# A six-layer decoder on one core: attention heads taken four at a time instead of two, and a new table of ticks

## The chip, the cores and the metric

The kernel runs on one core of a Trainium2 chip. The metric is the device time of one execution in microseconds. The five engines are named as the profile does: PE (TensorE), DVE (VectorE), ACT (ScalarE), POOL (GpSimd) and SP (SyncE, which here only issues transfers). Each runs its own list of instructions in order, and they meet at semaphores.

## The reference, cut to what matters

A batch of 8 sequences of 256 tokens and 256 features passes a memory read and a cross attention (the front, left alone by the change) and then six layers of this:

```
for i in range(6):
    x = attn_layer(shift_tokens(x), Wqkv[i], q_scale[i], k_scale[i], Wo[i]) + x
    x = ffn_layer(shift_tokens(x), ln_g[i], ln_b[i], W1[i], b1[i], W2[i], b2[i]) + x

attn_layer: q, k, v = split(x @ Wqkv)              # 16 heads of 64
            q, k = l2norm(q) * qs, l2norm(k) * ksc, then rotary tables
            sim = q . k * 8 within a window of 64 and the one before it
            out = softmax(masked sim) @ v;  out @ Wo
ffn_layer:  xn = layernorm(x) * g + b
            a, gate = split(xn @ W1 + b1)          # 682 columns each
            a * gelu(gate) @ W2 + b2
```

Everything is float32. A product with weights is made of three passes over a high and a low part of both factors (PASSES).

## The kernel before, in words

`layers` walks over 48 steps (6 layers times 8 sequences) and two at the ends. One step is a **slot**, and each slot n is a pipeline over three sequences: the 16 heads of step n are attended, the feed-forward part (FFN) of step n-1 is computed, and the second half of the projections of step n (group 1) and the first half of those of step n+1 (group 0) are made. A group is 8 heads, 512 columns.

A slot has 16 **ticks**, one for each head. In every engine's `slot` function a tick t first does its share of the heads and then walks over `SCHEDULE[t]`, a table written out by hand, whose items each engine turns into its own instructions in `dense`. So SCHEDULE sets the order on PE, ACT, DVE and POOL at once, and nothing is reordered at run time. The items:

- `("unit", g, u)`: one product of 512 columns for group g, on PE into one of two `project` banks (L791). u 0 to 3 are q and k of two token tiles; ACT squares and copies them out (L949, L950). u 4 and 5 are v (L954).
- `("rotate", g, u)`: DVE sums the squares, applies the tables (L1134 to L1141), POOL takes a power and, for k, scales (L1050 to L1059).
- `("turn", g, u)`: PE transposes the rotated q or k into a `project` bank, ACT copies it to qT or kT (L963). "unit" and "turn" and "input" take the two banks in turn, and PE waits in `bank_free` until ACT has read the use before last.
- `("project_out", t)`: the output projection of one token tile (L821). `("add_out",)`: DVE adds the residual (L1146); SP then shifts the tokens by three transfers.
- `norm_stats`, `norm_apply`, `norm_turn`: the layer norm. `("input",)`: the next sequence is transposed (L774), split by ACT and DVE.
- `("gate", i)`, `("value", i)`: a third of W1's gates or values each, into the single bank `wide` (L844). ACT applies Gelu to the gates (L982), DVE multiplies the values in (L1179), ACT makes the high part hT (L991 to L994), which is a single buffer and therefore waits until PE has made `("down", i-1)` from it (L859); `("low", i)` is its low part on DVE. `("residual",)`: L1195.

A head's own way, before the change, at tick t: at even t PE makes the scores of heads t and t+1 (`pair_scores`, L878, two banks, one for each side of a pair); DVE masks head t with the running minimum (L1215) at tick t; ACT takes the exponentials with their sums (L1019) in the same tick; at t+1 DVE inverts the sum (L1205) and scales (L1223); PE transposes a pair at each odd tick (`turn_pair`, L891), ACT copies it to probsT (L1004); at even ticks PE mixes the pair of two steps earlier with v (`pair_mix`, L905 to L909), ACT copies it to oT (L1012) and DVE makes its low part (L1228).

Gelu and the exponential are in different tables of ACT, so each slot loads a table twice (ACT_TABLE_LOAD at L982 and at L1019).

## Time and profile before

| | us |
|---|---|
| median of 3 runs | 3348.35 (3347.62 to 3349.45) |
| the profiled execution's own time | 3347.67 |
| its span | 3345.9 |
| busy in the span: PE, DVE, ACT, POOL | 2950.3, 2440.5, 2211.5, 1464.3 |
| mean granted clock of PE | 0.974 of 2.4 GHz |
| one slot in steady state | 62.4 |

The span runs from the first to the last instruction, so 1.8 us of the profiled execution lie around it. An engine's busy time counts its instructions; the rest is waiting. The idle time that stands with an instruction is what its engine waited just before it, and the name behind the arrow is the one that ended the wait. The chain that ended last has 44% on PE, 27% on DVE, 11% on ACT and 11% of issue.

### The profile page before, as it was taken

The numbers are of one execution on the slowest core, as the hardware profiler recorded it, in microseconds if no ns is written. First come the engines' busy times: TensorE is split into PE (matmuls) and PEld (weight loads), VectorE is DVE, ScalarE is ACT, GpSimd is POOL, SyncE is SP. The second block draws the span as 40 slices with busy tenths as digits, with TensorE's granted clock in tenths as the row PEclk, the third lists the DMA queues.
The fourth block names the chain that finished last, engine by engine and source line by source line (L and its number), as shares of the span: only waits on it lengthen the run. The fifth ranks groups of instructions, "written<-read, shape, count | busy, mean of one in ns | idle before, by whom it ended". The sixth has DMA issues, their size and how long they took to land.

```text
span 3345.9 us, 83253 instructions
## 1 busy us (share of the span) xinstructions
PE 2950.3 (88%) x26408; PEld 2463.4 (74%) x26408; DVE 2440.5 (73%) x8851; ACT 2211.5 (66%) x6256; POOL 1464.3 (44%) x1052
## 2 busy tenths in 40 slices
PE   6778998888999888999988999988999988898996
PEld 5567877777777767777776777766777767777775
DVE  3477777777777777777777777777777777777773
ACT  3357667666676666767666766766676666667663
POOL 3354454334444444445443444433544543454450
PEclk9899999999999999999999999999999999999997
DMA  4210010111001111100112010012101011110000
GB/s 136 68 40 23 17 30 22 40 57 53 22 17 30 42 50 49 30 22 17 30 53 71 18 30 22 17 40 76 35 20 27 24 41 48 35 32 27 27 26 21
DMA packets 109664, 124.10 MB, mean 37 GB/s; under 512 B 11589, under 2 KB 84129, under 8 KB 109473
## 3 DMA queue, kind: packets, MB, share of 16 engines
q1 hardware_dynamic: 109472, 121.75, 12.7%
q8 instruction: 95, 1.56, 0.2%
q14 instruction: 97, 0.79, 0.1%
HBM read 73.50 MB, written 16.78 MB: 27 GB/s over the span
## 4 chain that ended last, share of the span: by engine, by line
PE 44%; DVE 27%; ACT 11%; issue 11%; DMA 2%; DVEq 1%; POOL 1%; SPq 0%; ACTq 0%; POOLq 0%
PE project L791 12%; PE wide L844 7%; DVE with_sin L1137 6%; PE acc L859 6%; PE score L878 5%; DVE sums_sq L1134 4%; PE acc L821 4%; DVE probs L1215 4%; DVE probs L1223 3%; PE turned L891 2%; PE mix L905 2%; DVE sums_sq L1139 2%; ACT L982 2%; ACT with_sin L949 2%; ACT probs L1019 2%
## 5 line engine op out<-in xcount | busy, mean ns | idle before, releaser
L791 PE MATMUL project<-w_qkv,xT 128*128 128x512 f32 x3456 | 953.3, 415 | 37.8 <-DVE xT L1117 33.8
L1050 POOL TENSOR_TENSOR query_scale<-sums_sq,half 128x8 f32<-128x8 f32 x192 | 412.9, 2151 | 1230.8 <-DVE sums_sq L1139 1225.8
L1019 ACT ACTIVATE probs<-probs,shift 128x128 f32<-128x128 f32 x1536 | 605.4, 396 | 430.5 <-DVE shift L1215 425.2
L791 PEld LDWEIGHTS project<-w_qkv,xT 128*128 128x128 f32 x3456 | 628.2, 194 | 172.7 <-DVE xT L1117 41.9
L1215 DVE CUSTOM_DVE_ANT_0 probs<-score,mask,query_scale 128x128 f32<-128x128 f32 x1536 | 468.7, 342 | 304.1 <-PE score L878 290.3
L844 PE MATMUL wide<-nT,w_up 128*128 128x256 f32 x3456 | 493.6, 293 | 149.2 <-ACT gates L982 87.5
L844 PEld LDWEIGHTS wide<-nT,w_up 128*128 128x128 f32 x3456 | 444.5, 194 | 201.9 <-ACT gates L982 108.9
L1053 POOL TENSOR_TENSOR inv_norm<-sums_sq,half 128x8 f32<-128x8 f32 x192 | 411.2, 2141 | 224.5 <-DVE sums_sq L1139 223.1
L1223 DVE TENSOR_SCALAR probs<-probs,inv_sums 128x128 f32<-128x128 f32 x1536 | 381.5, 291 | 0.0
L1134 DVE TENSOR_REDUCE sums_sq<-with_sin 128x8 f32<-128x512 f32 x384 | 261.8, 682 | 78.8 <-ACT with_cos L950 78.6
L1137 DVE TENSOR_TENSOR with_sin<-with_cos,tables 128x512 f32<-128x512 f32 x384 | 301.9, 786 | 13.3
L878 PE MATMUL score<-kT,qT 64*64 64x128 f32 x6144 | 258.2, 283 | 53.7 <-DVE shift L1215 42.5
L1012 ACT CAST oT<-mix 128x256 fp32r<-128x256 f32 x384 | 143.8, 374 | 242.4 <-PE acc L821 142.3
L821 PE MATMUL acc<-w_out,oT 128*128 128x256 f32 x2304 | 296.3, 284 | 1.0 <-issue 1.0
L878 PEld LDWEIGHTS score<-kT,qT 64*64 64x64 f32 x6144 | 167.1, 133 | 167.4 <-issue 160.9
L1019 ACT ACTIVATION_READ_ACCUMULATOR probs<-probs,shift 128x1 f32 x1536 | 289.9, 189 | 0.0
L891 PE MATMUL turned<-ident,probs 128*128 128x128 f32 x1536 | 241.5, 280 | 44.9 <-DVE probs L1223 39.5
L821 PEld LDWEIGHTS acc<-w_out,oT 128*128 128x128 f32 x2304 | 277.1, 189 | 4.7 <-issue 1.2
L949 ACT ACTIVATE with_sin<-project 128x512 f32<-128x512 f32 x384 | 227.2, 592 | 76.5 <-PE project L791 76.5
L1141 DVE TENSOR_TENSOR with_cos<-with_cos,tables 128x512 f32<-128x512 f32 x384 | 265.9, 692 | 13.1
L859 PE MATMUL acc<-w_down,hT 128*128 128x256 f32 (+1 forms) x1728 | 246.1, 288 | 15.5 <-DVE hT L1190 11.2
L1004 ACT COPY probsT<-turned 128x512 f32<-128x512 f32 x384 | 226.1, 589 | 46.6 <-issue 39.9
(121 smaller groups left out, 5099.3 us busy)
## 6 DMA issues: line engine op xcount, KB each, us to landing
v_mid<-v SPq DMA_DIRECT2D x192, 128.0 KB, 2.3
staging<-in_w_qkv SPq DMA_DIRECT2D x24, 768.0 KB
y_in<-y_scratch SPq DMA_DIRECT2D x48, 256.0 KB, 2.8
res<-y_scratch SPq DMA_DIRECT2D x48, 256.0 KB, 2.7
y_scratch<-res SPq DMA_DIRECT2D x40, 256.0 KB, 2.4
staging<-in_w_up SPq DMA_DIRECT2D x12, 682.0 KB
staging<-in_w_out SPq DMA_DIRECT2D x6, 1024.0 KB
xn<-res SPq DMA_DIRECT2D x48, 112.0 KB, 2.3
```

The costliest lines, as they stand in the source:

```text
L791: last = pe.matmul(project[(x - 1) % 2][:], xT[a][:, h, t * P:(t + 1) * P], w_qkv[w][:, h, c, g, :], start=(h == 0 and (a, w) == PASSES[0] ...
L821: last = pe.matmul(acc[:, t, :], oT[a][:, p, t * P:(t + 1) * P], w_out[w][:, p, :], start=(p == 0 and (a, w) == PASSES[0]), stop=(p == PAI ...
L844: last = pe.matmul(wide[:, k, :], w_up[w][:, h, col:col + P], xnT[a][:, h, :], start=(h == 0 and (a, w) == PASSES[0]), stop=(h == HALVES - ...
L859: last = pe.matmul(acc[:, t, :], hT[a][0:rows, k, t * P:(t + 1) * P], w_down[w][0:rows, j, :], start=(j == 0 and t == 0 and (a, w) == PASS ...
L878: last = pe.matmul(score[side][sides[w % 2], (w // 2) * P:(w // 2 + 1) * P], qT[rows, pair, w * WINDOW:(w + 1) * WINDOW], kT[rows, pair, f ...
L1019: last = act.activation(probs[:, t % 4, cols], probs[:, t % 4, cols], ACT.Exp, bias=shift[:, t % 2, i:i + 1], scale=-1.0, accum_out=sums[: ...
L1050: pool.tensor_tensor(query_scale[:, u // 2, g * GROUP_HEADS:(g + 1) * GROUP_HEADS], sums_sq[:, u, :], half[:, 0:GROUP_HEADS], ALU.pow).the ...
L1053: pool.tensor_tensor(inv_norm[:, u // 2, :], sums_sq[:, u, :], half[:, 0:GROUP_HEADS], ALU.pow)
L1134: dve.tensor_reduce(sums_sq[:, u, :], with_sin[:, u, :].rearrange("p (h d) -> p h d", h=GROUP_HEADS), AXIS_X, ALU.add).then_inc(squares_su ...
L1137: dve.tensor_tensor(heads(with_sin[:, u, :]), heads(with_cos[:, u, :])[:, :, ::-1, :], table(2 * c + 1), ALU.mult)
L1215: last = dve.tensor_tensor_reduce(out=probs[:, t % 4, a:b], in0=score[t % 2][:, a:b], in1=mask[:, a:b], scale=query_scale[:, i, t:t + 1], ...
L1223: last = dve.tensor_scalar(probs[:, h4, a:b], probs[:, h4, a:b], inv_sums[:, h4, i:i + 1], None, ALU.mult)
```

## The change

1. **Heads in fours.** At every fourth tick PE makes the scores of four heads (`quad_scores`) and mixes the four heads before them (`quad_mix`). With q = t % 4: DVE masks heads 0 and 1 of the four at q = 0 and heads 2 and 3 at q = 1; ACT takes their exponentials in the same ticks; DVE scales 0 and 1 at q = 1, and 2 and 3 at q = 2; PE transposes 0 and 1 at q = 2 and 2 and 3 at q = 3. The four go to oT in one copy of 512 columns, at q = 0 on ACT and at q = 1 on DVE; the sums of two heads are inverted in one instruction. probsT holds four heads, shift four.
2. **A new SCHEDULE**, in which the output projection moves from ticks 3 and 4 to 1 and 2, the layer norm two ticks ahead, the gates from tick 9 to tick 7, and the rest with them.
3. **w_up without padding between its halves**, which pays for the larger probsT: the last tile of gates reads on into the next half, in rows that are not used later.
4. In SP's list the load of the tables at a layer's end moves behind the three shifting transfers.

```diff
 SCHEDULE = {
     0: [("unit", 1, 0)],
-    1: [("rotate", 1, 0), ("unit", 1, 1), ("rotate", 1, 1), ("unit", 1, 2)],
-    2: [("unit", 1, 3), ("rotate", 1, 2), ("turn", 1, 0)],
-    3: [("rotate", 1, 3), ("project_out", 0), ("turn", 1, 1)],
-    4: [("project_out", 1), ("turn", 1, 2), ("add_out",)],
-    5: [("unit", 1, 4)],
-    6: [("turn", 1, 3), ("unit", 1, 5), ("norm_stats",), ("input",)],
-    7: [("unit", 0, 0), ("norm_apply",)],
-    8: [("rotate", 0, 0), ("norm_turn",)],
-    9: [("unit", 0, 1), ("gate", 0), ("rotate", 0, 1), ("unit", 0, 2), ("gate", 1), ("unit", 0, 3), ("gate", 2)],
-    10: [("rotate", 0, 2), ("turn", 0, 0)],
-    11: [("value", 0), ("rotate", 0, 3), ("turn", 0, 1), ("unit", 0, 4), ("low", 0)],
-    12: [("value", 1), ("down", 0), ("turn", 0, 2), ("low", 1)],
-    13: [("value", 2), ("down", 1), ("turn", 0, 3), ("low", 2)],
-    14: [("down", 2)],
-    15: [("unit", 0, 5), ("residual",)],
+    1: [("unit", 1, 1), ("rotate", 1, 0), ("project_out", 0)],
+    2: [("rotate", 1, 1), ("project_out", 1), ("unit", 1, 2)],
+    3: [("add_out",), ("rotate", 1, 2), ("unit", 1, 3), ("turn", 1, 0)],
+    4: [("norm_stats",), ("rotate", 1, 3), ("turn", 1, 1)],
+    5: [("unit", 1, 4), ("norm_apply",), ("unit", 1, 5), ("turn", 1, 2)],
+    6: [("norm_turn",), ("turn", 1, 3), ("input",), ("unit", 0, 0)],
+    7: [("gate", 0), ("unit", 0, 1), ("gate", 1), ("rotate", 0, 0), ("gate", 2)],
+    8: [("rotate", 0, 1), ("unit", 0, 2)],
+    9: [("value", 0), ("unit", 0, 3)],
+    10: [("rotate", 0, 2), ("value", 1), ("turn", 0, 0), ("low", 0)],
+    11: [("down", 0), ("value", 2), ("rotate", 0, 3), ("turn", 0, 1), ("low", 1)],
+    12: [("low", 2), ("turn", 0, 2)],
+    13: [("down", 1), ("unit", 0, 4)],
+    14: [("down", 2), ("turn", 0, 3), ("unit", 0, 5)],
+    15: [("residual",)],
 }
...
-                    if t % 2 == 0 and s.head(t, 0) is not None:
-                        pair_scores(s, t, s.head(t, 0))
-                    if t % 2 == 0 and s.head(t, 4) is not None:
-                        pair_mix(s.n, (t - 4) % HEADS, s.head(t, 4), s.n * PAIRS + (t - 4) // 2)
-                    if t % 2 == 1 and s.head(t, 2) is not None:
-                        turn_pair((t - 2) % HEADS, s.head(t, 2))
+                    q = t % QUAD_HEADS
+                    if q == 0 and s.head(t, 0) is not None:
+                        quad_scores(s, t, s.head(t, 0))
+                    if q == 0 and s.head(t, 4) is not None:
+                        quad_mix(s.n, (t - 4) % HEADS, s.head(t, 4), s.n * PAIRS + (t - 4) // 2)
+                    if q == 2 and s.head(t, 2) is not None:
+                        turn_pair(0, s.head(t, 2))
+                    if q == 3 and s.head(t, 3) is not None:
+                        turn_pair(2, s.head(t, 3) + 2)
...
+                    k = 2 * (q % 2)
+                    H = s.head(t, q)
+                    if H is not None and q < 2:
+                        for j in range(k, k + 2):
+                            act.wait_ge(scores_masked, H + j + 1)
...
+                            last.then_inc(exp_done, 1)
+                    if H is not None and q >= 2:
+                        act.wait_ge(probs_turned, H + k + 2)
+                        wait(act, mixed, H)
+                        act.copy(probsT[:, k:k + 2, :].rearrange("p a b -> p (a b)"), turned[:]).then_inc(probsT_copied, 2)
...
-                        act.copy(oT[0][:, pair, :], mix[:, pair % 2, :]).then_inc(out_high, 1)
+                        act.copy(oT[0][:, pair:pair + 2, :], mix[:]).then_inc(out_high, 2)
...
+                    if H is not None and q in (1, 2):
+                        dve.wait_ge(exp_done, H + done + 2)
+                        dve.reciprocal(inv_sums[:, done:done + 2, :], sums[:, done:done + 2, :]).then_inc(sums_inverted, 2)
+                    if H is not None and q < 2:
...
+                        dve.wait_ge(scores_ready, H + QUAD_HEADS)
+                        wait(dve, probs_turned, H)
+                        for k in (2 * q, 2 * q + 1):
...
+                            last.then_inc(scores_masked, 1)
+                    if H is not None and q in (1, 2):
...
+                    if q == 1 and s.head(t, 5) is not None:
+                        pair = ((t - 5) % HEADS) // 2
+                        dve.wait_ge(out_high, s.n * PAIRS + (t - 5) // 2 + 2)
+                        dve.tensor_tensor(oT[1][:, pair:pair + 2, :], mix[:], oT[0][:, pair:pair + 2, :].bitcast(FP32),
+                                          ALU.subtract).then_inc(out_split, 2)
```

How the order moves, first on ACT at ticks 5 and 6 (exponentials, then v out of its banks, then qT). Before, tick 5 and the start of tick 6:

```order
L1019 ACTIVATE probs,sums<-probs,shift 128x128 [waits scores_masked]
L1019 ACTIVATE probs,sums<-probs,shift 128x128
L942 REGISTER_ALU
L954 COPY v<-project 128x512 [waits mixed,filled]
L1012 CAST oT<-mix 128x256 [waits mixed]
```

With the change, tick 5:

```order
L1018 ACTIVATE probs,sums<-probs,shift 128x128 [waits scores_masked]
L1018 ACTIVATE probs,sums<-probs,shift 128x128
L1015 REGISTER_ALU
L1018 ACTIVATE probs,sums<-probs,shift 128x128 [waits scores_masked]
L1018 ACTIVATE probs,sums<-probs,shift 128x128
L951 REGISTER_ALU
L963 COPY v<-project 128x512 [waits mixed,filled]
L951 REGISTER_ALU
L963 COPY v<-project 128x512 [waits mixed,filled]
L968 REGISTER_ALU
L972 COPY qT<-project 128x4x128 [waits scores_ready,filled]
```

Two heads' exponentials, and no longer one head's, stand ahead of the copy of v, and the second v and a turn stand in the same tick.

Second, PE at the same place, ticks 5 and 6 with the change (the two units of v, then "turn" 1, 2, then a pair of heads turned, the norm's transposes):

```order
L795 MATMUL project<-w_qkv,xT 128x512 [waits act_read]
L795 MATMUL project<-w_qkv,xT 128x512 x5
L95 REGISTER_ALU
L795 MATMUL project<-w_qkv,xT 128x512 [waits act_read]
L795 MATMUL project<-w_qkv,xT 128x512 x5
L804 REGISTER_ALU
L95 REGISTER_ALU [waits parts_ready]
L813 MATMUL project<-ident,with_cos 128x128 [waits act_read]
L814 MATMUL project<-ident,with_sin 128x128
```

Before, a score, a mix and a turned pair of heads stood around a single unit at this place:

```order
L891 MATMUL turned<-ident,probs 128x128 x3
L93 REGISTER_ALU
L791 MATMUL project<-w_qkv,xT 128x512 [waits act_read]
L791 MATMUL project<-w_qkv,xT 128x512 x5
L93 REGISTER_ALU
L878 MATMUL score<-kT,qT 64x128 [waits scores_masked]
L878 MATMUL score<-kT,qT 64x128 x7
```

So "turn" 1, 2 is now the third use of a bank in a row, and waits for a read that ACT makes after four activations.

Third, ACT at ticks 11 to 12, the cast of the last third of hT and what follows it. Before, ticks 13 and 14:

```order
L993 CAST hT<-gates 128x256 [waits h_used]
L994 CAST hT<-gates 42x256
L959 REGISTER_ALU
L963 COPY kT<-project 128x4x128 [waits scores_ready,filled]
L1012 CAST oT<-mix 128x256 [waits mixed]
```

With the change:

```order
L1002 CAST hT<-gates 128x256 [waits h_used]
L1003 CAST hT<-gates 42x256
L968 REGISTER_ALU
L972 COPY kT<-project 128x4x128 [waits scores_ready,filled]
L1015 REGISTER_ALU
L1018 ACTIVATE probs,sums<-probs,shift 128x128 [waits scores_masked]
L1018 ACTIVATE probs,sums<-probs,shift 128x128
```

The cast waits on h_used, which PE gives after ("down", 1). Before, that item was in the same tick as the cast (13); now the cast is in tick 11 and ("down", 1) in tick 13, behind a score, a mix and a turn.

## Rows read from the trace of the kernel before

**Rows 1.** The page's first part: busy time and share of PE.

```profile
PE 2950.3 (88%) x26408; PEld 2463.4 (74%) x26408; DVE 2440.5 (73%) x8851; ACT 2211.5 (66%) x6256; POOL 1464.3 (44%) x1052
```

**Rows 2.** One steady slot: stretch, its length, busy of each engine, PEclk, DMA, GB/s.

```profile
1501.30:1563.70 62.40, 57.81 (x541) 48.56 (x540) 47.49 (x179) 43.64 (x125) 29.16 (x20) 1.00 0.09 23
```

**Rows 3.** Timeline of DVE, the residual additions alone: start, us, line, operation.

```profile
604.99 0.69 DVE L1195 TENSOR_TENSOR res<-acc,res 128x512 f32<-128x512 f32 x1
...
820.89 0.68 DVE L1195 TENSOR_TENSOR res<-acc,res 128x512 f32<-128x512 f32 x1
...
1472.11 0.68 DVE L1195 TENSOR_TENSOR res<-acc,res 128x512 f32<-128x512 f32 x1
...
1534.51 0.69 DVE L1195 TENSOR_TENSOR res<-acc,res 128x512 f32<-128x512 f32 x1
```

**Rows 4.** Timeline of PE: start, us, what, and the idle time before it with its releaser.

```profile
1506.60 1.68 PE L844 MATMUL wide<-nT,w_up 128*128 128x256 f32 x12 [1.19 <-DVE nT L1169]
...
1511.04 1.69 PE L844 MATMUL wide<-nT,w_up 128*128 128x256 f32 x12 [1.37 <-ACT gates L982]
```

**Rows 5.** Timeline of PE where it waits for nothing: starts show what each takes.

```profile
1535.56 0.67 PE L878 MATMUL score<-kT,qT 64*64 64x128 f32 x16
1536.16 0.44 PE L905 MATMUL mix<-probsT,v 128*64 128x128 f32 x4
...
1536.76 1.66 PE L791 MATMUL project<-w_qkv,xT 128*128 128x512 f32 x6
1538.25 0.60 PE L891 MATMUL turned<-ident,probs 128*128 128x128 f32 x4
...
1545.55 3.06 PE L821 MATMUL acc<-w_out,oT 128*128 128x256 f32 x24
```

**Rows 6.** Timeline of ACT behind the unit of rows 5.

```profile
1538.53 0.60 ACT L949 ACTIVATE with_sin<-project 128x512 f32<-128x512 f32 x1 [0.47 <-PE project L791]
1539.02 0.58 ACT L950 COPY with_cos<-project 128x512 f32<-128x512 f32 x1
...
1539.97 0.42 ACT L1019 ACTIVATE probs<-probs,shift 128x128 f32<-128x128 f32 x1
...
1540.75 0.60 ACT L949 ACTIVATE with_sin<-project 128x512 f32<-128x512 f32 x1
```

**Rows 7.** Timeline of DVE: values, a head masked and scaled, rotations, norm statistics.

```profile
1520.76 0.87 DVE L1179 SCALAR_TENSOR_TENSOR gates<-wide,params,gates 128x256 f32<-128x256 f32 x2
...
1536.52 0.35 DVE L1215 CUSTOM_DVE_ANT_0 probs<-score,mask,query_scale 128x128 f32<-128x128 f32 x1 [0.65 <-PE score L878]
...
1537.07 0.48 DVE L1223 TENSOR_SCALAR probs<-probs,inv_sums 128x128 f32<-128x128 f32 x2
1537.46 0.42 DVE L1228 TENSOR_TENSOR oT<-mix,oT 128x256 fp32r<-128x256 f32 x1
...
1539.64 0.69 DVE L1134 TENSOR_REDUCE sums_sq<-with_sin 128x8 f32<-128x512 f32 x1 [0.17 <-ACT with_cos L950]
...
1541.86 0.69 DVE L1134 TENSOR_REDUCE sums_sq<-with_sin 128x8 f32<-128x512 f32 x1
...
1559.16 0.29 DVE L1153 BATCH_NORM_STATS2 ln_stats<-res 128x6 f32<-128x128 f32 x1 [0.18 <-DMA xn<-res]
```

**Rows 8.** Timeline of ACT: the table load and the first two Gelu.

```profile
1508.85 1.28 ACT L982 ACT_TABLE_LOAD   x1
1510.15 0.84 ACT L982 ACTIVATE gates<-wide,params 128x256 f32<-128x256 f32 x2
```

**Rows 9.** Timeline of ACT: the last third of hT.

```profile
1530.24 0.41 ACT L993 CAST hT<-gates 128x256 fp32r<-128x256 f32 x1 [0.53 <-PE acc L859]
```

**Rows 10.** Timeline of PE: the same forms as in rows 4 and 5 behind longer waits.

```profile
219.06 0.89 PE L806 MATMUL project<-ident,with_cos 128*128 128x128 f32 x4 [2.12 <-POOL with_cos L1059]
...
724.32 2.79 PE L844 MATMUL wide<-nT,w_up 128*128 128x256 f32 x12 [2.57 <-ACT gates L982]
...
755.62 1.13 PE L878 MATMUL score<-kT,qT 64*64 64x128 f32 x16 [2.53 <-ACT v L954]
```

127 lines of the change are left out of this document (56 added, 71 removed).

## The prediction, made before the changed kernel was run

> **What bounds the kernel now.** I read the page first. PE is busy in 88% of the span, DVE in 73%, ACT in 66% [rows 1]. Then the stretches: in a steady slot of 62.4 us PE is busy for 57.8 at the full granted clock, DVE for 47.5 and ACT for 43.6 [rows 2]. Then the timeline of PE, which repeats from slot to slot: the residual additions are 62.4 apart [rows 3]. What PE issues without waiting is read from the starts [rows 5]: scores of a pair of heads 0.6, mix of a pair 0.6, a unit 1.5, a turned pair of heads 0.4, one tile of the output projection 2.9 (24 matmuls of 3.06 with the overlap taken off); the six groups of `wide` and three of `down` take 1.5 each (the first row of rows 4 with its overlap off). A slot has 12 units (17.9), 9 such groups (13.5), two projection tiles (5.8), 8 pairs scored and mixed (9.6), 8 turned (3.2), and 56 transposes of q, k, the input and the norm at 0.11, the rate of rows 5's turned pair (6.2): 56.2 us. So in each slot PE loses only 6.2 us, in short waits such as the 1.19 and 1.37 around the gates [rows 4] with what each drains. **PE bounds it, and a perfect order could give 10% at most.** DVE and ACT have 15 and 19 us of slack, but they are in order, so what matters is what stands ahead of the instruction that PE waits for.
>
> **What the edits save by themselves.** Per slot: four copies to oT of 512 columns for eight of 256, four subtractions likewise, eight inversions for sixteen. That is 1 to 2 us less on ACT and as much on DVE, beside PE, and nothing on PE, which issues the same matmuls. The missing padding of w_up and SP's moved load change no duration: the same 128 columns are read, and the table load is wanted only at a layer's end; cover gone, it would cost one transfer in five switches, under 3 us each. I take 0.
>
> **What the order does.** I walk one steady slot with these steps. DVE: a head masked 0.55, scaled 0.4, a rotation 2.2 (1539.64 to 1541.86), a value group 0.8, norm statistics 1.3 (estimate from six instructions of the kind shown), 512 columns subtracted 0.6 to 0.7 [rows 7, 3]. ACT: a head's exponentials 0.8, square and copy together 1.0, other copies of 512 columns 0.5 and 0.6 until seen [rows 6]. What PE makes is seen 0.3 after its last issue (rows 5's unit is issued by 1538.25, ACT starts at 1538.53 [rows 6]). Time 0 is where PE starts the scores of tick 0.
>
> Tick 1. The scores are seen at 1.5, heads 0 and 1 are masked by 2.6, ACT has their exponentials at 3.8. DVE then inverts, masks heads 2 and 3, scales 0 and 1, and only then makes the low part of oT: 6.7. PE has scored and mixed (2.4) and made two units (5.4) and waits there for ("project_out", 0): **1.3 us**. Before, this item came two ticks later and waited for nothing.
>
> Ticks 1 to 5. PE has 11.6 us from there to the end of the scores of tick 4 (two projection tiles, two units, two turned pairs, one turn, the scores), so 18.3. DVE idles meanwhile, since the unit of rotation 1,2 comes behind both projection tiles. Then everything is due at once. DVE: heads 4 and 5 masked (to 19.7), norm statistics (21.0), rotation 1,3 (23.2), inversion and head 6 masked, seen at 23.9. ACT: exponentials of 6 and 7 (25.5), and only then the copy of v out of unit 1,4: 26.2. PE has finished both units of v at 23.5 (0.5 lost for its bank) and needs that bank for ("turn", 1, 2): **2.7 us**, behind the 0.5.
>
> Ticks 5 to 7. The turn, a turned pair and the norm's transposes end at 27.9. ACT then copies a turned pair, makes the norm's two activations and cast (1.6), empties turn 1,3 and both input halves, with DVE subtracting, before unit 0,0 may start at 31.8. PE's own work in it is 0.9: **3.1 us** lost. Then gate 0; its Gelu needs the table load and 0.84 [rows 8]; with one unit between, PE waits 1.0, and for gate 2, with nothing between, 1.1: **2.1 us**. The same two places cost 1.37 and nothing before.
>
> Ticks 8 to 11. DVE masks two heads, rotates 0,1, masks two, scales two, makes oT's low part and then value 0, at 50.1 when the scores began at 41.9. PE waits 1.0 for value 1, and then 1.8 for ("down", 0), whose low part stands behind a rotation and value 1, and 0.3 for ("down", 1): **3.1 us**.
>
> Ticks 11 to 14. ACT casts the last third of hT only after ("down", 1). Such a wait was 0.53 when both were in one tick [rows 9]. Now PE makes the scores, the mix and a turn of tick 12 first, and DVE a rotation and the low part: `down` 1 ends at 63.5 as ACT sees it. Behind the cast on ACT stand turn 0,1 and the exponentials of heads 12 to 15, so PE waits 1.5 for a bank and 2.3 for the scaled heads 12 and 13: **3.8 us**.
>
> Sum: 16.5 us of waits beside 56.2 of work, **72.7 for a slot, 10.3 more than now**, at the full clock. The slot closes: at 72.7 the scores of the next can start, and DVE and ACT are free by then.
>
> **PE's clock.** The rows show that after 2.57 us without work a group of `wide` took 2.79 and not 1.69, after 2.53 the scores 1.13 and not 0.67, after 2.12 four transposes 0.89 and not 0.60 [rows 10, 4, 5]: the half level, 1.2 GHz. After waits to 1.4 nothing of the kind shows in steady slots, whose granted clock is 1.00 [rows 2]. The changed slot has 2.7 us without work in tick 5 and then some 5.5 us with little of it up to unit 0,0. At half rate the turn, the turned pair and the norm's transposes take 1.7 more, turn 1,3 and an input half 0.6, unit 0,0 1.4 and the pair behind it 0.4, all on the path: about 4 us, so 76.7. The wait of 2.3 in tick 14 may do the same to `down` 2 and what follows (2.5 more: 79.2).
> The Trainium skill, "TensorE: Matmul & The Clock Gate", section on HAM oscillation, says that a kernel whose PE waits between bursts falls to half rate and pays for it in each burst. By that rule every slot would pay the 4 us; without it the sum below would be 3825. The trace agrees where the waits are long (rows 10).
>
> **The sum.** From the first to the last residual addition there are 47 intervals: 30 of 62.4, 15 around the five layer switches (each three 215.9, 604.99 to 820.89 [rows 3]) and two at the end. I take 14.3 more for each of the 30 (429), 10.3 for each of the 15 (155; these already pay for a slow clock, as at 724.32 and 755.62 [rows 10]), and 13 for the start and the end together, where half of the work is missing (from below 0, from above twice 14). 3347.7 of the profiled execution + 597 = **3945 us**; the median of the runs shown is 0.7 above that execution, which changes nothing.
>
> **The rivals.**
> *The chain as walked, at full clock.* Against it stand rows 10, for it that the clock kept up through shorter waits. 45 x 10.3 + 13: 3825. Chance 0.18.
> *Two falls per slot.* 30 x 16.8 + 155 + 13: 4020; with the switches paying too, 4095. Chance 0.27.
> *The waits are shorter than walked.* A step may be overlapped that I put in a row; with half of the growth at full clock, 3590, with three quarters 3705. Chance 0.07.
> *PE stays the bound and the order helps.* This needs what the change seems made for: DVE and ACT free when PE asks, and the waits at gates all that is left. Its place is tick 5: if ACT emptied unit 1,4 before the exponentials of heads 6 and 7, and DVE rotated beside them. A slot would be 56.2 + 2.1 at the gates and about 1 for draining, 59.3: 3.1 less in 45 intervals, 3208. It decides from where the waits of a slot sum to under 6.2. For it speaks DVE's and ACT's slack [rows 2], against it that both are in order. Chance 0.06. That the change does nothing measurable I give 0.02: it moves every wait.
> My forecast, one fall per slot, has 0.40.
>
> **The range.** 3700 to 4095: from three quarters of the growth to two falls with the switches. Left out are most of the short-wait case, the faster one, and anything beyond two falls, somewhat under 0.2. A measurement of this kernel tells 0.2% (7 us) from no change. Faster 0.06, same 0.02, slower 0.92.
>
> **What would show it.** In the changed profile: residual additions about 77 apart; busy times of ACT and DVE within 3% of now; "turn" 1,2 of PE (L813) waiting 2 to 3 us for ACT's v; the cast of hT (L1002) waiting some 5 us for PE's acc, and not 0.5; the turned pair (L897) waiting about 2 for DVE; the output projection (L825) waiting 1 to 1.5 for oT; the gates waiting 1 us twice; the granted clock well under 1.00 in each slot after the turn of tick 5, at full level otherwise. The forecast is wrong if those waits are there but short, if the clock stays at 1.00, or if the period is below 62.4; then DVE's or ACT's steps overlap in a way that rows 6 and 7 don't show.

## The result and the profile after

| | before | after |
|---|---|---|
| median, us | 3347.98 (4 runs, 3344.40 to 3349.45) | 4112.62 (4 runs, 4104.88 to 4124.02) |
| ratio to before | | 1.2289, 95% interval 1.2254 to 1.2323 |
| span of the profiled execution | 3345.9 | 4105.4 |
| busy PE, DVE, ACT, POOL | 2950.3, 2440.5, 2211.5, 1464.3 | 3167.5, 2436.6, 2157.4, 1448.5 |
| mean granted clock | 0.974 | 0.904 |
| one steady slot (mean of 30) | 62.4 | 77.0 |
| three intervals at a switch of layers (mean of 5) | 214.0 | 272.3 |

The change made the kernel 23% slower. The forecast was 3945 with a range up to 4095: right in its direction, and too low by 168 us, so that the result lies outside the range.

The page's first part, which answers to [rows 1]. PE does the same 26408 matmuls and is busy 217 us longer; DVE and ACT do no more work than before.

```profile
PE 3167.5 (77%) x26408; PEld 2676.1 (65%) x26408; DVE 2436.6 (59%) x8275; ACT 2157.4 (53%) x6064; POOL 1448.5 (35%) x1052
```

The stretches of the changed kernel (stretch, length, busy of PE, PEld, DVE, ACT and POOL, granted clock, DMA share, GB/s): two steady slots, which answer to [rows 2], and the three intervals at the first switch.

```profile
2362.50:2440.20 77.70, 63.66 (x541) 53.87 (x541) 47.90 (x165) 42.46 (x121) 28.78 (x20) 0.92 0.07 19
2440.20:2516.00 75.80, 59.15 (x542) 49.53 (x541) 47.96 (x165) 42.36 (x121) 28.78 (x20) 0.98 0.07 19
692.50:792.50 100.00, 74.38 (x586) 63.39 (x586) 55.38 (x182) 50.48 (x136) 29.01 (x20) 0.81 0.11 34
792.50:884.40 91.90, 69.88 (x552) 59.98 (x544) 53.66 (x177) 48.03 (x133) 29.11 (x20) 0.81 0.17 52
884.40:969.80 85.40, 61.49 (x503) 52.52 (x496) 49.30 (x170) 41.90 (x121) 28.78 (x20) 0.86 0.13 38
```

The same three intervals in the kernel before, in the same columns:

```profile
605.00:682.40 77.40, 63.02 (x544) 51.81 (x543) 56.74 (x195) 50.23 (x139) 29.12 (x20) 0.94 0.15 44
682.40:754.00 71.60, 60.93 (x542) 50.28 (x541) 54.50 (x189) 48.90 (x137) 29.38 (x20) 0.97 0.21 66
754.00:820.90 66.90, 59.84 (x536) 49.99 (x537) 48.62 (x182) 44.14 (x128) 29.11 (x20) 0.95 0.18 51
```

In the two steady slots PE is busy 61.4 us on average, 3.6 more than in [rows 2] for the same matmuls, which is the slower clock, and idle for 15.4 against 4.6: 10.8 us of new waits. Over all 30 steady slots the two are 3.9 (61.7 against 57.9 busy) and 10.7 (15.3 against 4.6 idle). The timeline of DVE, residual additions alone, answers to [rows 3]:

```profile
692.48 0.69 DVE L1206 TENSOR_TENSOR res<-acc,res 128x512 f32<-128x512 f32 x1 [0.76 <-PE acc L863]
...
969.75 0.69 DVE L1206 TENSOR_TENSOR res<-acc,res 128x512 f32<-128x512 f32 x1 [2.37 <-PE acc L863]
...
2440.25 0.69 DVE L1206 TENSOR_TENSOR res<-acc,res 128x512 f32<-128x512 f32 x1 [0.76 <-PE acc L863]
...
2516.06 0.69 DVE L1206 TENSOR_TENSOR res<-acc,res 128x512 f32<-128x512 f32 x1 [0.88 <-PE acc L863]
```

The first pair spans a switch, 277.3 us where before had 215.9; the five switches take 277.3, 276.6, 272.4, 272.6 and 262.9. The account from the residual additions of both traces: 30 steady intervals grew by 14.6 (437), 15 at switches by 19.5 (292, that is 5 x 58.4), the first addition came 11.3 later, and the last two intervals are 126.1 and not 106.8 (19.3). The sum is 759.5, and so is the difference of the spans.

Now the waits of one steady slot, in the timeline of PE (start, us, what, idle time before it and its releaser). The scores of tick 0 start at 2366.22.

```profile
2372.94 3.10 PE L825 MATMUL acc<-w_out,oT 128*128 128x256 f32 x24 [1.58 <-DVE oT L1243]
...
2388.07 1.66 PE L795 MATMUL project<-w_qkv,xT 128*128 128x512 f32 x6 [0.57 <-ACT kT L972]
2392.03 0.33 PE L813 MATMUL project<-ident,with_cos 128*128 128x128 f32 x1 [2.30 <-ACT v L963]
...
2397.55 0.44 PE L778 MATMUL project<-ident,y_in 128*128 128x128 f32 x2 [1.15 <-ACT kT L972]
2399.09 2.50 PE L795 MATMUL project<-w_qkv,xT 128*128 128x512 f32 x6 [1.09 <-DVE xT L1128]
...
2406.47 1.70 PE L848 MATMUL wide<-nT,w_up 128*128 128x256 f32 x12 [0.89 <-ACT gates L991]
2409.09 1.68 PE L848 MATMUL wide<-nT,w_up 128*128 128x256 f32 x12 [0.93 <-ACT gates L991]
...
2418.45 0.66 PE L897 MATMUL turned<-ident,probs 128*128 128x128 f32 x4 [1.21 <-DVE probs L1238]
2419.84 2.76 PE L848 MATMUL wide<-nT,w_up 128*128 128x256 f32 x12 [0.73 <-DVE gates L1190]
...
2434.11 1.68 PE L795 MATMUL project<-w_qkv,xT 128*128 128x512 f32 x6 [1.28 <-ACT kT L972]
2437.95 0.66 PE L897 MATMUL turned<-ident,probs 128*128 128x128 f32 x4 [2.16 <-DVE probs L1238]
```

With one of 0.15 they sum to 14.04, all that PE is idle in this slot. A unit (`project<-w_qkv,xT` x6) takes 2.50 after the waits around tick 5, where 1.66 is the full rate, and a value group 2.76 and not 1.69 after those of ticks 9 and 10: half clock for most of each. The stretches around tick 5 show it (same columns as above):

```profile
2392.00:2396.00 4.00, 3.97 (x21) 3.67 (x22) 2.94 (x12) 2.29 (x5) 1.10 (x1) 0.59 0.29 66
2396.00:2400.00 4.00, 1.76 (x8) 1.11 (x7) 1.54 (x3) 2.11 (x5) 1.42 (x2) 0.93 0.00 0
2400.00:2404.00 4.00, 4.00 (x20) 3.51 (x20) 1.23 (x2) 1.56 (x3) 0.00 (x0) 0.63 0.00 0
```

### The profile page after: what moved, and what is told of

It reads as the page before. It is cut to its first block, busy times and chain, and to the rows that moved or that the text cites. A ratio compares the mean times of both kernels' runs of the same rounds, so it can differ in the third digit from the quotient of the medians.

```text
span 4105.4 us, 82137 instructions
## 1 busy us (share of the span) xinstructions
PE 3167.5 (77%) x26408; PEld 2676.1 (65%) x26408; DVE 2436.6 (59%) x8275; ACT 2157.4 (53%) x6064; POOL 1448.5 (35%) x1052
## 4 chain that ended last, share of the span: by engine, by line
PE 47%; DVE 25%; issue 12%; ACT 10%; DVEq 1%; POOL 1%; ACTq 0%; DMA 0%; SPq 0%; POOLq 0%
PE project L795 10%; PE wide L848 10%; PE acc L825 7%; PE acc L863 6%; DVE probs L1229 5%; PE turned L897 4%; DVE probs L1238 4%; ACT probs L1018 4%; PE score L885 3%; DVE with_sin L1148 3%; DVE sums_sq L1145 2%; DVE gates L1190 2%; DVE oT L1243 2%; PE project L813 2%; ACT gates L991 1%
## 5 line engine op out<-in xcount | busy, mean ns | idle before, releaser
L795 PE MATMUL project<-w_qkv,xT 128*128 128x512 f32 x3456 | 1006.8, 433 | 145.8 <-ACT kT L972 91.6
L795 PEld LDWEIGHTS project<-w_qkv,xT 128*128 128x128 f32 x3456 | 662.1, 204 | 314.1 <-ACT kT L972 121.4
L848 PE MATMUL wide<-nT,w_up 128*128 128x256 f32 x3456 | 534.6, 310 | 124.6 <-ACT gates L991 88.5
L848 PEld LDWEIGHTS wide<-nT,w_up 128*128 128x128 f32 x3456 | 488.7, 212 | 172.9 <-ACT gates L991 119.3
L897 PE MATMUL turned<-ident,probs 128*128 128x128 f32 x1536 | 285.0, 317 | 235.3 <-DVE probs L1238 235.2
L1238 DVE TENSOR_SCALAR probs<-probs,inv_sums 128x128 f32<-128x128 f32 x1536 | 430.0, 343 | 6.8
L897 PEld LDWEIGHTS turned<-ident,probs 128*128 128x128 f32 x1536 | 219.9, 165 | 308.2 <-DVE probs L1238 278.9
L1145 DVE TENSOR_REDUCE sums_sq<-with_sin 128x8 f32<-128x512 f32 x384 | 258.8, 674 | 272.6 <-ACT with_cos L959 272.6
L813 PE MATMUL project<-ident,with_cos 128*128 128x128 f32 x768 | 206.4, 303 | 113.0 <-ACT v L963 113.0
L863 PEld LDWEIGHTS acc<-w_down,hT 128*128 128x128 f32 (+1 forms) x1728 | 236.0, 204 | 82.1 <-DVE hT L1198 69.1
L1148 DVE TENSOR_TENSOR with_sin<-with_cos,tables 128x512 f32<-128x512 f32 x384 | 266.2, 693 | 13.3
```

The lines of the kernel that those rows point to most:

```text
L795: last = pe.matmul(project[(x - 1) % 2][:], xT[a][:, h, t * P:(t + 1) * P], w_qkv[w][:, h, c, g, :], start=(h == 0 and (a, w) == PASSES[0] ...
L848: last = pe.matmul(wide[:, k, :], w_up[w][:, h * W1_COLS + col:h * W1_COLS + col + P], xnT[a][:, h, :], start=(h == 0 and (a, w) == PASSES ...
L863: last = pe.matmul(acc[:, t, :], hT[a][0:rows, k, t * P:(t + 1) * P], w_down[w][0:rows, j, :], start=(j == 0 and t == 0 and (a, w) == PASS ...
L897: last = pe.transpose(turned[:, (TILES * side + i) * P:(TILES * side + i + 1) * P], pr[:, i * P:(i + 1) * P], ident[:])
L1145: dve.tensor_reduce(sums_sq[:, u, :], with_sin[:, u, :].rearrange("p (h d) -> p h d", h=GROUP_HEADS), AXIS_X, ALU.add).then_inc(squares_su ...
L1148: dve.tensor_tensor(heads(with_sin[:, u, :]), heads(with_cos[:, u, :])[:, :, ::-1, :], table(2 * c + 1), ALU.mult)
```

## The experiments

For each kernel the table gives what the residual additions of its trace say: a steady interval (mean of 30), three intervals at a switch (mean of 5), and the **excess** of these over three steady ones. Each is read from one trace, and the steady slots of the changed kernel differ by up to 3.7 us among themselves, so a few tenths between its variants say little.

| kernel | median | ratio, 95% interval | steady | switch | excess |
|---|---|---|---|---|---|
| before | 3347.98 | | 62.4 | 214.0 | 26.6 |
| after | 4112.62 | 1.2289 [1.2254, 1.2323] | 77.0 | 272.3 | 41.3 |
| e1, fours alone | 3711.92 | 1.1073 [1.1041, 1.1105] | 70.2 | 236.8 | 26.2 |
| e2, table alone | 3819.31 | 1.1393 [1.1360, 1.1426] | 72.3 | 245.7 | 28.9 |
| e3, PE kept busy | 4065.59 | 1.2128 [1.2092, 1.2163] | 76.4 | 267.1 | 37.8 |
| e4, cast late | 3925.99 | 1.1711 [1.1667, 1.1755] | 73.8 | 256.4 | 35.1 |
| e5, v early | 4135.11 | 1.2367 [1.2316, 1.2418] | 77.7 | 273.9 | 40.8 |
| e45, both | 3927.35 | 1.1746 [1.1696, 1.1795] | 73.8 | 255.9 | 34.6 |
| e6, after with thin splits | 4043.86 | 1.2094 [1.2034, 1.2155] | 77.7 | 257.2 | 24.2 |
| e7, before with thin splits | 3278.38 | 0.9805 [0.9754, 0.9855] | 62.4 | 200.4 | 13.1 |
| e8, projection later | 4140.60 | 1.2378 [1.2345, 1.2410] | 77.8 | 275.2 | 41.8 |
| e9, rotation last | 4015.16 | 1.2003 [1.1982, 1.2024] | 75.1 | 264.7 | 39.3 |
| e10, before with gates covered | 3333.11 | 0.9962 [0.9949, 0.9975] | 62.3 | 210.5 | 23.5 |
| e11, splits moved | 4068.18 | 1.2151 [1.2061, 1.2241] | 77.4 | 264.6 | 32.3 |

### Which part of the change costs: e1 and e2

**e1: heads in fours, the old table.** The changed kernel with the SCHEDULE of the kernel before.

> The changed kernel with the SCHEDULE of before; heads still in fours. If the new table makes the loss (my theory), most of the 765 us go: 3350 to 3600. If the grain of four heads makes it (rival), the time stays above 3900. In between both have a share.

Measured 3711.92, between the two, so both parts have a share. **e2: the new table, heads in pairs.** The kernel before with the new SCHEDULE, with these items where its pairs and its cast can use them, the ffn's splits from tick 13 on, and the moved load of the tables:

```diff
-    1: [("unit", 1, 1), ("rotate", 1, 0), ("project_out", 0)],
-    2: [("rotate", 1, 1), ("project_out", 1), ("unit", 1, 2)],
-    3: [("add_out",), ...
+    1: [("unit", 1, 1), ("rotate", 1, 0)],
+    2: [("rotate", 1, 1), ("unit", 1, 2)],
+    3: [("project_out", 0), ("project_out", 1), ("add_out",), ...
-    11: [("down", 0), ("value", 2), ...("low", 1)], 12: [("low", 2), ("turn", 0, 2)], 13: [("down", 1), ("unit", 0, 4)]
+    11: [("down", 0), ...("low", 1)], 12: [("turn", 0, 2)], 13: [("value", 2), ("down", 1), ("unit", 0, 4), ("low", 2)]
```

> The kernel of before, heads in pairs, with the new table as near as pairs allow: both output projections in tick 3 (the last pair's low part is ready only after tick 2), the value group 2 and its cast in tick 13 with down 1, the weight splits of the up projection from tick 13 on, the tables' load behind the shifts. If the table makes the loss: 3700 to 3950. If the fours make it: 3350 to 3500.

Measured 3819.31, in the range of "the table makes the loss". But each part costs alone, 7.8 and 9.8 us a slot; together 14.6. The reading, argued from the orders above: the fours put two heads' masks and exponentials ahead of whatever a tick's items need, the table puts those items where they are needed at once. With fours under the old table the gates wait, for DVE's norm and for Gelu; the timeline of PE in e1:

```profile
1656.57 1.67 PE L848 MATMUL wide<-nT,w_up 128*128 128x256 f32 x12 [2.56 <-DVE nT L1180]
...
1661.78 2.93 PE L848 MATMUL wide<-nT,w_up 128*128 128x256 f32 x12 [2.14 <-ACT gates L991]
```

With pairs under the new table the waits of tick 5 are there all the same; the timeline of PE in e2:

```profile
1086.05 0.33 PE L809 MATMUL project<-ident,with_cos 128*128 128x128 f32 x1 [2.18 <-ACT v L954]
1091.65 0.44 PE L774 MATMUL project<-ident,y_in 128*128 128x128 f32 x2 [2.08 <-ACT kT L963]
```

So the turn of tick 5 waits because of its place, not because of the fours. And the excess at a switch is that of the kernel before in e1 and near it in e2 (26.2 and 28.9): only both together raise it. (In e2 the ffn's splits stand later too; e4 below has fours, the table and the splits in those places, and its excess is 35.1.)

### What the clock costs: e3

The changed kernel with matmuls of no use, whose result is overwritten, in PE's gaps of ticks 5 and 6:

```diff
+            def filler(f, count):
+                pe.wait_ge(acc_read, f * 2 + 1 + 1)
+                for k in range(count):
+                    pe.matmul(acc[:, k % 2, :], oT[0][:, 0, 0:P], w_out[0][:, 0, :], start=True, stop=True)
...
+                    if s.ffn and (g, u) == (1, 2):
+                        filler(f, 18)
...
+                    if s.ffn:
+                        filler(f, 12)
```

> The changed kernel, where PE makes 18 more matmuls of 256 columns into the idle acc bank before turn 1,2 and 12 more before the input's transposes (results unused), some 2 and 1.5 us at full rate, inside the two long waits of ticks 5 and 6. If the half clock after those waits costs about 4 us a slot, the added work keeps the clock up and the time FALLS, by 2.5 to 4 us in each of some 45 slots: 3930 to 4010, a steady period of 73 to 74.5. If the clock is not the cost, nothing or worse: 4110 to 4200.

The time, 4065.59, is in neither range. The clock did stay up where it was filled (1.00 from 2360 to 2380 in e3): the turn waited 0.18 and not 2.30, and the unit behind the input takes 1.67 and not 2.50. But the slot fell by 0.6 only. The half clock behind the waits of ticks 9 and 10 is there as without filling, in about every second slot (2.85 here, 2.76 in the slot shown above). The timeline of PE in e3:

```profile
2365.30 0.33 PE L822 MATMUL project<-ident,with_cos 128*128 128x128 f32 x1 [0.18 <-ACT v L972]
...
2371.91 1.67 PE L802 MATMUL project<-w_qkv,xT 128*128 128x512 f32 x6 [1.09 <-DVE xT L1137]
...
2391.07 2.85 PE L857 MATMUL wide<-nT,w_up 128*128 128x256 f32 x12 [0.72 <-DVE gates L1199]
```

The means of the 30 steady slots say where the rest went. PE idles 12.3 and not 15.3; the matmuls of no use are busy for 4.0, which is 1.0 more than the waits that they took; and all others are busy for 60.2 and not 61.7. So filling gave back 1.5 of the 3.9 us that the slow clock costs and lost 1.0 by its own length. The other 2.4 of the clock lie elsewhere in the slot, and nothing was filled there. In all it gave 47 us of 4112.

### Ticks 11 to 14 and 4 to 6: e4, e5, e45, e9

**e4** has the last value group, its low part and the cast of hT two ticks later, so that the cast no longer waits in front of the exponentials of heads 12 to 15; the ffn's splits of ticks 11 and 12 move with it.

```diff
-    11: [("down", 0), ("value", 2), ("rotate", 0, 3), ("turn", 0, 1), ("low", 1)],
-    12: [("low", 2), ("turn", 0, 2)],
-    13: [("down", 1), ("unit", 0, 4)],
+    11: [("down", 0), ("rotate", 0, 3), ("turn", 0, 1), ("low", 1)],
+    12: [("turn", 0, 2)],
+    13: [("value", 2), ("down", 1), ("unit", 0, 4), ("low", 2)],
```

> The changed kernel with value 2 and low 2 in tick 13 beside down 1 (and the up projection's weight splits from tick 13 on). If ACT's cast behind down 1 holds back the exponentials of heads 12 to 15, the waits of 1.3 and 2.2 us in ticks 13 and 14 go, and part comes back in tick 13 and 14 itself for value 2 and down 2: 3 to 5 us less in a slot, 3890 to 3980. If those waits only hide a DVE that is late anyway: 4080 to 4130.

As the first theory said: 3925.99. The waits for kT and for the turned pair (1.28 and 2.16) are gone, and 0.39 for probsT and 0.73 for hT are in their place. Here the walk named the cause rightly.

**e5** moves ("unit", 1, 4) from the start of tick 5 to the end of tick 4, so that ACT copies v before the exponentials of heads 6 and 7. **e45** has both edits.

> The changed kernel with unit 1,4 moved from tick 5 to the end of tick 4, so that ACT empties it before the exponentials of heads 6 and 7. If turn 1,2 waits for that copy and for nothing else: the 2.3 us go and the half clock of ticks 5 and 6 with them in part, 4 to 6 us a slot, 3840 to 3930. If the wait only moves to the norm's transposes (DVE's norm_apply ends 0.6 later than that copy) and the input's chain, 0 to 2 us: 4020 to 4112.

> The changed kernel with both moves, the cast of the last third late and unit 1,4 early. If the waits are separate, the gains of the two runs add up, to 3650 to 3850; if one chain of DVE feeds both, the sum is less than the two.

Nothing gained: 4135.11, above both ranges, and 3927.35, e4's time. The wait for v is gone, and what stood behind it waits instead, as the timeline of PE in e5 shows:

```profile
2407.83 0.66 PE L897 MATMUL turned<-ident,probs 128*128 128x128 f32 x4 [1.67 <-DVE probs L1238]
2409.66 0.65 PE L835 MATMUL wide<-ident,xn 128*128 128x128 f32 x4 [1.17 <-DVE xn L1175]
```

Both wait for DVE, whose list in ticks 4 and 5 is masks, norm statistics, rotation 1,3, masks, scaling, low part, norm. **e9** is e45 with ("rotate", 1, 3) moved behind all that, to the end of tick 5.

> The changed kernel with the cast late (as in e4_cast_late), ('unit', 1, 4) at the end of tick 4, and ('rotate', 1, 3) moved from tick 4 to the end of tick 5, behind the norm and 'turn' 1,2. It differs from e45_both (3927) by the rotation's place alone. Theory A (in ticks 4 to 6 DVE's order sets PE's waits: masks, statistics, rotation, masks, scale, oT, norm): the turned pair in tick 6 and the norm's transposes come about 2 us sooner, 'turn' 1,3 is ready in time or waits under 1 us more: 3800 to 3880. Theory B (the rotation is wanted as soon as the norm, its power and scale on POOL take 6 us, so 'turn' 1,3 takes over the wait): 3920 to 4000.

4015.16, 88 us worse than e45 and 15 above the second theory's range; 41 of the 88 lie in the steady slots and 44 at the switches. The two waits for DVE are gone, and a longer one for POOL, which makes a rotation's power and products, takes their place. The timeline of PE in e9:

```profile
2417.45 1.11 PE L810 MATMUL project<-ident,with_cos 128*128 128x128 f32 x4 [5.31 <-POOL with_cos L1070]
```

So in ticks 4 to 6 two chains end nearly together, DVE's norm and the rotation through POOL. Whichever is put first, PE waits for the other. More of PE's work between them, or the old distance of two ticks, should cover both; no run tried it.

### Where the excess at a switch comes from: e6, e7, e8, e11

At a switch ACT and DVE also convert ("split") the next layer's weights, a few pieces after the items of some ticks. **e6** and **e7** are the changed kernel and the kernel before with one column of each piece converted from the second layer on; the weights of these layers are therefore not the reference's.

```diff
-            last = act.copy(high, raw)
+            last = act.copy(high, raw) if isinstance(layer, int) else act.copy(high[:, ..., 0:1], raw[:, ..., 0:1])
...
-            last = dve.tensor_tensor(low, raw, high.bitcast(FP32), ALU.subtract)
+                last = dve.tensor_tensor(low[:, ..., 0:1], raw[:, ..., 0:1], high[:, ..., 0:1].bitcast(FP32), ALU.subtract)
```

> The changed kernel where the weight splits of the next layer convert one column of each row of a piece only (the weights of layers 1 to 5 are then wrong); waits and order stay. If the work of the splits on ACT and DVE lies on the chain in the changed kernel (my reading of the switch intervals, 277 for three, against 230 for three steady ones), nearly all of 47 us per switch goes: 3870 to 3930. If it is the transfers or the clock: 4050 to 4110.

> The kernel before with the same thinning of the weight splits. Its switches cost 28.6 us each over steady slots. If that is the splits' work too, 3200 to 3240; if it is transfers, 3320 to 3348. Against the run of the changed kernel it tells whether the same splits cost more there: 18 us more per switch if the order has no slack for them.

Measured 4043.86 and 3278.38, each between its two ranges. The bulk of the splits costs 17.2 us per switch in the changed kernel and 13.5 in the one before; a difference of 3.6 explains little of the 14.7 by which the excess grew. Without bulk the changed kernel's switch still has 11.0 more. **e8** moves the output projection one tick later:

```diff
-    1: [("unit", 1, 1), ("rotate", 1, 0), ("project_out", 0)],
-    2: [("rotate", 1, 1), ("project_out", 1), ("unit", 1, 2)],
-    3: [("add_out",), ...
+    1: [("unit", 1, 1), ("rotate", 1, 0)],
+    2: [("rotate", 1, 1), ("project_out", 0), ("unit", 1, 2)],
+    3: [("project_out", 1), ("add_out",), ...
```

> The changed kernel with ('project_out', 0) moved from tick 1 to tick 2 and ('project_out', 1) from tick 2 to tick 3. In the changed kernel's trace the first waits 1.58 us for oT's low part in a steady slot, and once in a switch of layers 9.29 us, at 898.07, while DVE stands with 'issue' for 3.24 and 3.28 us in front of its masks. Theory A (this item in tick 1 is what the excess of the switch intervals comes from): steady slots 0.5 to 1.6 shorter, and the three switch intervals fall from 277.2 to 262 to 270: 4112 - 45 x 1 - 5 x 7 = about 4010 to 4050. Theory B (the stall of DVE comes through whatever stands next, and the later unit 1,2 and rotation cost what is saved): 4080 to 4120, with the wait on other lines and the three intervals within 3 us of 277.

4140.60, Theory B and 21 us above its range: the projection waits no more (1.58), the turned pair behind it waits 0.92, and the clock takes back more than was won (over the steady slots PE idles 0.9 less and is busy 1.6 more). The excess is unchanged, 41.8. **e11** moves the splits alone:

```diff
-    "projections": {0: [(0, 0), (0, 1)], 3: [(0, 2), (0, 3)], 4: [(0, 4), (0, 5)],
-                    8: [(1, 0)], 9: [(1, 1)], 11: [(1, 2)], 12: [(1, 3)], 13: [(1, 4)], 14: [(1, 5)]},
-    "ffn": {7: [(2, 0), (2, 1)], 8: [(2, 2), (2, 3)], 11: [(3, 0), (3, 1)], 12: [(3, 2)], 13: [(4, 0), (4, 1)],
-            14: [(4, 2), (5, 0)], 15: [(5, 1), (5, 2)]},
+    "projections": {1: [(0, 0), (0, 1)], 2: [(0, 2), (0, 3)], 5: [(0, 4), (0, 5)],
+                    9: [(1, 0)], 10: [(1, 1), (1, 2)], 13: [(1, 3)], 14: [(1, 4), (1, 5)]},
+    "ffn": {9: [(2, 0), (2, 1)], 10: [(2, 2), (2, 3)], 13: [(3, 0), (3, 1), (3, 2)], 14: [(4, 0), (4, 1), (4, 2)],
+            15: [(5, 0), (5, 1), (5, 2)]},
```

> The changed kernel with another table of splits (the pieces of the next layer's weights that ACT and DVE convert at a switch): none behind ticks 0, 3, 4, 7, 8, 11 and 12 any more, all behind ticks with t % 4 of 1 or 2 and behind 15. In the changed kernel's trace DVE stands 8.03 us at 840.98 in front of a split, and four masks, the inversion, the scaling and the low part come behind it, while PE waits 4.79 for the turned pair at 850.83; with heads in fours the work of a head that PE waits for is bunched in the two ticks after every fourth. The three intervals at a switch have 272.3 on average over the five switches, 41.3 more than three steady ones; in the kernel before 26.7. Theory A (the excess that the forecast missed comes from splits that stand ahead of the bunched masks): the excess falls to 25 to 33, 4112 - 5 x 12 = 4020 to 4070, steady slots unchanged. Theory B (it comes from waits of all kinds and the clock, wherever the splits stand): the excess stays at 37 to 45, 4090 to 4130.

As Theory A said, the excess fell to 32.3, and the steady slots stayed (77.4): 9.0 of the 14.7 hang on where the splits stand (7.8, if the switch intervals are compared directly). The median fell by 44, with its two runs 25 apart (4055.71 and 4080.65), so the trace's intervals are the better measure. The timeline of DVE and then of PE in the changed kernel, second interval of the switch: behind tick 7 DVE stands in front of a split, and the masks of tick 8 follow it.

```profile
840.98 1.29 DVE L243 TENSOR_TENSOR w_out<-staging,w_out 128x512 fp32r<-128x512 f32 x2 [8.03 <-ACT w_out L237]
842.18 0.35 DVE L1229 CUSTOM_DVE_ANT_0 probs<-score,mask,query_scale 128x128 f32<-128x128 f32 x1
```

```profile
850.83 1.11 PE L897 MATMUL turned<-ident,probs 128*128 128x128 f32 x4 [4.79 <-DVE probs L1238]
...
874.67 1.12 PE L897 MATMUL turned<-ident,probs 128*128 128x128 f32 x4 [6.23 <-DVE probs L1238]
898.07 4.46 PE L825 MATMUL acc<-w_out,oT 128*128 128x256 f32 x24 [9.29 <-DVE oT L1243]
```

PE's timeline in e11: the 4.79 of tick 10 became 1.20, the 6.23 of tick 14 became 2.18, and the wait in front of the projection 6.29, with new ones of 1.90 in tick 11 and of 5.86 behind the slot's end, which shows no releaser.

```profile
839.51 0.66 PE L897 MATMUL turned<-ident,probs 128*128 128x128 f32 x4 [1.20 <-DVE probs L1238]
...
845.36 0.66 PE L897 MATMUL turned<-ident,probs 128*128 128x128 f32 x4 [1.90 <-DVE probs L1238]
...
865.12 0.66 PE L897 MATMUL turned<-ident,probs 128*128 128x128 f32 x4 [2.18 <-DVE probs L1238]
875.72 1.99 PE L885 MATMUL score<-kT,qT 64*64 64x128 f32 x32 [5.86 <-issue]
889.73 5.47 PE L825 MATMUL acc<-w_out,oT 128*128 128x256 f32 x24 [6.29 <-DVE oT L1243]
```

The excess can be taken apart further with the traces of these five kernels: into PE's busy and idle time, and by switch. `run_slots` loops over five layers, so four of the five switches end in the loop's jump back, and the fifth leaves the loop.

| excess, us | mean of 5 | of it PE busy | of it PE idle | the four with a jump back | the fifth |
|---|---|---|---|---|---|
| before | 26.6 | 9.1 | 17.5 | 27.0 | 25.3 |
| after | 41.3 | 16.2 | 25.1 | 43.7 | 31.9 |
| e11, splits moved | 32.3 | 14.4 | 17.9 | 33.6 | 27.0 |
| e6, after with thin splits | 24.2 | 11.9 | 12.3 | 26.3 | 15.4 |
| e7, before with thin splits | 13.1 | 4.5 | 8.6 | 13.9 | 10.2 |

Moving the splits brings PE's idle part back to what it was before the change (17.9 against 17.5), and at the fifth switch nearly the whole excess (27.0 against 25.3). What it leaves, 5.7, is nearly all PE busy for longer with the same matmuls (14.4 against 9.1), and most of it lies at the four switches with a jump back (33.6 against 27.0). There both kernels have waits with no releaser, shown at the end of this text: DVE's two add up to 6.5 to 7.7 us in the changed kernel, and the kernel before has 2.5 to 4.5. No run took them away, so that they slow PE's clock behind them is a reading and not shown.

### A better kernel: e10

The kernel before with the gates' waits covered by items of the next tick:

```diff
-    9: [("unit", 0, 1), ("gate", 0), ("rotate", 0, 1), ("unit", 0, 2), ("gate", 1), ("unit", 0, 3), ("gate", 2)],
-    10: [("rotate", 0, 2), ("turn", 0, 0)],
+    9: [("unit", 0, 1), ("gate", 0), ("rotate", 0, 1), ("unit", 0, 2), ("unit", 0, 3), ("gate", 1), ("turn", 0, 0), ("gate", 2)],
+    10: [("rotate", 0, 2)],
```

> The kernel before with one edit in tick 9: ('unit', 0, 3) stands between ('gate', 0) and ('gate', 1) beside unit 0,2, and ('turn', 0, 0) between ('gate', 1) and ('gate', 2). The gates' waits in the kernel before are 1.19 and 1.37 us in a slot, the second for Gelu behind the table load. Theory A (PE bounds that kernel, and a wait taken from it comes back whole): 1.0 to 1.4 less in each of some 45 slots, 3285 to 3310. Theory B (the wait comes again at the next item, gate 2 or the rotation's turn, since ACT's copies of two units now stand ahead of the Gelu): 3340 to 3400, and the wait stands at gate 2 or at 'turn' 0,0.

3333.11 in six runs, ratio 0.9962 with an interval below 1: faster than both kernels, by 0.4%. It is between the two theories. The wait of 1.37 at gate 1 is 0.11, but a steady slot is 62.3: the time is waited for at the next pair that DVE has to scale, and at hT. The timeline of PE in e10:

```profile
1515.38 0.66 PE L891 MATMUL turned<-ident,probs 128*128 128x128 f32 x4 [0.71 <-DVE probs L1223]
...
1522.36 1.68 PE L859 MATMUL acc<-w_down,hT 128*128 128x256 f32 x12 [0.26 <-DVE hT L1187]
```

The gain comes from the switches (5 x 3.5 less) and 0.1 in each steady interval, against 8 more at the ends.

## Why the prediction was wrong

**What bounds it and what the edits save: right.** PE's idle time became 15.3 us a slot with DVE and ACT as busy as before (2436.6 and 2157.4, within 3% of before). The fewer instructions saved nothing in time. On ACT they took 1.2 us off a steady slot, as forecast; on DVE nothing (47.9 against 47.6), since two scalings in each slot now take 1.07 longer (the last section).

**The walk through a slot: right in most of its places and in its total.** It gave 72.7 at full clock (its waits, as listed, sum to 16.6 and not 16.5); the trace has 14.0 of waits in one kind of slot, where 16.5 were walked, and 16.7 in the other, beside 57.8 of busy time at the full clock of [rows 2] (56.2 in the walk): 71.8 and 74.5, 73.1 on average. In its order, for the first kind: the projection 1.3, measured 1.58; the bank 0.5, measured 0.57; the turn of tick 5 2.7, measured 2.30; the norm and the input 3.1, measured 2.24 (1.15 and 1.09); the gates 2.1, measured 1.82; ticks 8 to 11 3.1, measured 2.09 (of which 1.21 is a turned pair that the walk had without a wait, while its 1.8 in front of ("down", 0) is missing here and 1.51 in the other kind of slot); ticks 11 to 14 3.8, measured 3.44. The cast of hT waits for PE 5.21 and 4.17, with 0.53 in [rows 9]. The timeline of ACT:

```profile
2426.06 0.62 ACT L1000 CAST hT<-gates 128x512 fp32r<-128x512 f32 x1 [4.17 <-PE acc L863]
2432.86 0.40 ACT L1002 CAST hT<-gates 128x256 fp32r<-128x256 f32 x1 [5.21 <-PE acc L863]
```

That a wait was at the right place did not make its named cause the only one. The copy of v behind the exponentials was called the cause of the turn's 2.7; e5 took it away and gained nothing, since DVE's order and the rotation through POOL end at the same time. The faster rival's point, that v emptied early would free tick 5, falls with that. The cast in tick 11 was a cause, and e4 took back 187 us with it (its splits moved as well, and 31 of these lie at the switches: 5 times the 6.2 by which its excess is smaller).

**One fall of the clock per slot: right in size, not in form.** 4 us were taken; busy time grew by 3.9. But slots alternate between more of it and less (63.66 and 59.15 us busy), the granted clock falls a second time in about every second slot, in ticks 9 and 10, and taking the fall of ticks 5 and 6 away gave back 1.5 (e3).

**The steady term: right.** 14.3 was taken for each of the 30, 14.6 measured: 8 us in all.

**The term of the 15 intervals at switches: wrong, and this is the step that failed.** It took 10.3 for each, "these already pay for a slow clock". They grew by 19.5, which is 137 of the 168 us (the steady intervals give 8, the ends 18, and the profiled execution lies 5 under the median). Two errors are in it. The intervals did pay the clock once more: PE's busy time in the three at a switch is 201.3 on average where it was 182.7, a growth of 18.6 where three steady slots have 11.6. At the first switch it is 205.8 (74.38, 69.88, 61.49) where it was 183.8, with the clock at 0.81, 0.81 and 0.86 where it was 0.94, 0.97 and 0.95. A slow clock in some instructions is no reason that others are not slowed too. Taking the steady 14.3 there alone would have given 60 more, 4005. And on top came 14.7 per switch that no steady slot has, 7.0 of it PE busy and 7.7 PE idle. The walk was of a slot without splits; no term held what happens to a split when the heads' work behind it is bunched. e11 took back 9.0 of the 14.7, and nearly all of the idle part, by moving the splits; e6 and e7 show that their bulk is 3.6 of it. The other 5.7 are nearly all PE's slower clock, mostly at the four switches with the loop's jump back, where DVE stands with "issue" in front of it; why the clock is lower there stays open, since neither was taken away by itself.

**The ends: too small.** 13 was taken, from bounds of 0 and 28; the trace has 30.6 (11.3 ahead of the first addition, 19.3 in the last two intervals), so the upper bound was too low as well. Some of the 11.3 may be variation: e7, which is the kernel before up to its first addition, has it 2.5 later.

**The rivals.** The nearest was "two falls with the switches paying too", 4095, and the range ended there. Its own terms, 16.8 for each of 45 intervals and 13 for the ends, give 3347.7 + 756 + 13 = 4117 and not 4095: with the sum done right the range would have held the measured time. That would have been luck in part, since steady slots grew by 14.6 and not 16.8, and the switches by 19.5.

## What to carry to other kernels

When a slot of a pipeline is walked and its growth multiplied, the rare slots with extra work (a change of layer, the ends) want a walk of their own: here a third of the intervals gave 38% of the loss, and were priced at half of it. In a schedule of in-order engines that all walk one table, ask of a wait which second chain ends just behind it, before the instruction in front is called its cause: of five moves that each took a seen wait away, e4 gave back much, e10 a little, and e5, e8 and e9 nothing or less. Bunching work (four heads at once) leaves DVE's and ACT's busy times nearly alone and lengthens what stands in front of the items that come due just behind it. And a sum that sets the end of a range deserves to be added twice.
